# Weight blocks m, n, r first, and the state vectors' layers between the steps of tile 0's softmax

## The reference

```python
# L0: modulated attention over the heads of one token (16 heads of 32)
def modulated_linear(x, s, aff_w, aff_b, w, b):
    style = s @ aff_w.T + aff_b
    w_mod = w[None] * style[:, None, :]
    w_mod = w_mod * rsqrt(sum(w_mod * w_mod, axis=2) + EPS)[:, :, None]
    return einsum('bni,boi->bno', x, w_mod) + b
kx = modulated_linear(x, s, k...).reshape(B, N, H, D)
A = softmax(einsum('bnhd,bnjd->bnhj', kx, kx) / sqrt(D))
x = x + modulated_linear(einsum('bnhj,bnjd->bnhd', A, kx).reshape(B, N, F), s, o...)

# L1: six branches, concatenated
h = _ln(_ln(x, pw_g[pathway_ids], pw_b[pathway_ids]), cp_g[...], cp_b[...])
t = _ln(x, tm_g[time_steps], tm_b[time_steps])
m = x + _mlp_ln(memory_state, mem...)[:, None, :]      # n: noise, r: resource likewise
s = _ln(x, ms_g[scale_type], ms_b[scale_type])
w = softmax(aw)
cat = concatenate([w[0] * h, w[1] * t, w[2] * m, w[3] * n, w[4] * r, w[5] * s])
x = x + _mlp_ln(cat, int_W1, int_b1, int_W2, int_b2, int_g, int_be)
```

## Time and profile before

| | |
|---|---|
| Time, median of 3 runs | 870.54 us (870.13 to 871.36) |
| Profiled execution: its time, its span | 869.47 us, 867.6 us |
| Busy: PE, PEld | 836.8 us (96%), 731.9 us (84%) |
| Busy: DVE, ACT, POOL | 646.7 (75%), 487.6 (56%), 605.7 us (70%) |
| Chain that ended last, by engine | PE 88%, DVE 5%, DMA 2%, POOL 2%, ACT 1%, issue 1% |
| Mean granted TensorE clock | 0.989 of full speed |

### The profile page before, as it was taken

One profiled execution on the slowest core, in us unless ns is written; L12 is line 12 of the kernel. 1 busy time (PEld: TensorE's weight loads), 2 busy tenths in 40 slices (PEclk: granted clock), 3 DMA queues, 4 the chain that ended last, 5 costly groups with the idle time before them and its releaser, 6 DMA issues.

```text
span 867.6 us, 19685 instructions
## 1 busy us (share of the span) xinstructions
PE 836.8 (96%) x7456; PEld 731.9 (84%) x7474; DVE 646.7 (75%) x1067; ACT 487.6 (56%) x851; POOL 605.7 (70%) x766
## 2 busy tenths in 40 slices
PE   5996999999999999999999999999999999999997
PEld 5853888988889898888989898888988898898986
DVE  3589778778786867678797877679797767677652
ACT  3567555565656465465656556465647546464531
POOL 2367998778786767768776866668787775756472
PEclk9998999999999999999999999999999999999999
DMA  8972233424343333525243332424343342323110
GB/s 277 419 268 62 71 91 105 126 63 150 83 151 81 98 93 86 128 51 158 71 149 89 107 93 69 127 68 145 83 123 91 87 117 49 104 68 83 47 50 25
DMA packets 104365, 95.55 MB, mean 110 GB/s; under 512 B 72880, under 2 KB 78160, under 8 KB 102608
## 3 DMA queue, kind: packets, MB, share of 16 engines
q1 hardware_dynamic: 95056, 69.26, 27.7%
q0 software_dynamic: 4608, 16.78, 7.1%
q10 hardware_dynamic: 4608, 8.25, 2.8%
HBM read 69.60 MB, written 8.40 MB: 90 GB/s over the span
## 4 chain that ended last, share of the span: by engine, by line
PE 88%; DVE 5%; DMA 2%; POOL 2%; issue 1%; ACT 1%; ACTq 0%; another core or an unknown queue 0%; DVEq 0%; POOLq 0%
PE acc L405 43%; PE tok L405 28%; PE att L405 8%; PE xp L558 6%; PE xp L405 3%; DMA kb<-in_kb 1%; DVE stg_e L1284 1%; DMA pgb<-in_pw,pidx 1%; DVE raw_k L1170 0%; DVE W1xl L1274 0%; POOL op0l L1706 0%; DVE qt L1290 0%; POOL W2l L1710 0%; DVE q L1297 0%; DVE BD L1185 0%
## 5 line engine op out<-in xcount | busy, mean ns | idle before, releaser
L1706 POOL TENSOR_TENSOR op1l<-ytmp,op1h 128x512 fp32r<-128x512 f32 x64 | 89.8, 1403 | 20.1 <-ACT op1h L912 19.6
L1652 POOL TENSOR_TENSOR xlo<-xraw,xhi 128x512 fp32r<-128x512 f32 x31 | 40.5, 1306 | 68.0 <-ACT xhi L804 68.0
L405 PE MATMUL acc<-op0h,W1xh 128*128 128x256 f32 x256 | 75.8, 296 | 1.4 <-DVE op0l L1376 1.1
L405 PE MATMUL acc<-op1h,W1th 128*128 128x256 f32 x256 | 75.0, 293 | 0.0
L405 PE MATMUL acc<-op1h,W1hh 128*128 128x256 f32 x256 | 73.7, 288 | 0.0
L405 PE MATMUL acc<-op0h,W1sh 128*128 128x256 f32 x256 | 73.7, 288 | 0.0
L405 PE MATMUL acc<-op1h,W1tl 128*128 128x256 f32 x256 | 72.4, 283 | 0.0
L405 PE MATMUL acc<-op1l,W1hh 128*128 128x256 f32 x256 | 72.4, 283 | 0.0
L405 PE MATMUL acc<-op1l,W1th 128*128 128x256 f32 x256 | 72.4, 283 | 0.0
L405 PE MATMUL acc<-op0h,W1sl 128*128 128x256 f32 x256 | 72.4, 283 | 0.0
L405 PE MATMUL acc<-op1h,W1hl 128*128 128x256 f32 x256 | 72.4, 283 | 0.0
(11 more groups left out here) (269 smaller groups left out, 3005.2 us busy)
## 6 DMA issues: line engine op xcount, KB each, us to landing
xsq<-in_x SPq DMA_DIRECT2D x32, 256.0 KB, 3.1
xb<-in_x SPq DMA_DIRECT2D x32, 256.0 KB, 3.0
out<-xb SPq DMA_DIRECT2D x32, 256.0 KB, 2.4
BD<-q SPq DMA_DIRECT2D x124, 64.0 KB, 2.1
BD<-v SPq DMA_DIRECT2D x124, 64.0 KB
xraw<-in_xT SPq DMA_DIRECT2D x30, 256.0 KB, 3.0
ring<-in_k_wT ACTq DMA_DIRECT2D x6, 256.0 KB, 3.3
dmb<-dm_rows SPq DMA_DIRECT2D x6, 256.0 KB, 3.9
```

Source lines behind the costliest of these rows:

```text
L405: return e.matmul(o, a, b, start=start, stop=True, skip_group_check=True)
L1652: e.tensor_tensor(xlo[:, :, :], (xraw1 if g == 1 else xraw)[:, :, :], xhi[:, :, :].bitcast(F32), ALU.subtract).then_inc(s["xlo"], 1)
L1706: e.tensor_tensor(op[slot]["l"][:, :, half(g)], four(ytmp[YT[n, g][0]]), op[slot]["h"][:, :, half(g)].bitcast(F32), ALU.subtract).then_inc ...
```

## The change

The first-layer weights `mlp1` get a place of their own (`mlp_w1`, where the low part of `W2` is put later); block n goes straight to `stg["a"]`. The transfers of m and n go right behind that of the output weights, r behind the first-layer weights. TensorE does `mlp1` right after `proj(0)`, `mlp2` and the transposes of the demodulation behind `mod_rows(1)`, and the tables of t, s, h in three pieces; `proj(2)` follows the tables of m, n, r. ScalarE does `x_scaled`, the silu and the gain tables ahead of score_low(0). VectorE does six of the eight `x_weights` around the scores of tile 0 and the vectors ahead of `mod_first(1)`. ScalarE's split of t goes ahead of `q_hi(2)` and `e_first(1)`; GpSimd's split of t begins before root1(0).

```diff
@@
         raw["o"] = raw_o
+        mlp_w1 = at("mlp_w1", [128, 4, 512], offset=place["W2l"])
         stg = {n: at(f"stg_{n}", [128, 4, 512], offset=place[f"W{w}h"]) for n, w in zip("abcde", ("1x", "1t", "1s", "1h", "2"))}
@@
             e.dma_start(raw["o"][:, :, :], A["o_wT"]).then_inc(s["c_wo"], 16)
+            e.dma_start(raw["x"][:, :, :], A["int_w1"][2]).then_inc(s["c_rm"], 16)
+            e.dma_start(stg["a"][:, :, :], A["int_w1"][3]).then_inc(s["c_rn"], 16)
             load_sq(1)
-            e.dma_start(stg["a"][:, :, :], A["mlp1"]).then_inc(s["c_m1"], 16)
+            e.dma_start(mlp_w1[:, :, :], A["mlp1"]).then_inc(s["c_m1"], 16)
+            e.dma_start(raw["r"][:, :, :], A["int_w1"][4]).then_inc(s["c_rr"], 16)
             for i, n in enumerate(("mem", "noi", "res")):
                 e.dma_start(stg["bcd"[i]][:, :, :], A[n + "_w2"]).then_inc(s["c_w2"], 16)
-            e.dma_start(raw["x"][:, :, :], A["int_w1"][2]).then_inc(s["c_rm"], 16)
+            e.wait_ge(s["tq"], 1)
+            for i in range(3):
+                e.dma_start(rv[i][:, :], A["rows_v"][i]).then_inc(s["c_rv"], 16)
             e.dma_start(raw["t"][:, :, :], A["int_w1"][1]).then_inc(s["c_rt"], 16)
             e.dma_start(raw["s"][:, :, :], A["int_w1"][5]).then_inc(s["c_rs"], 16)
             e.dma_start(raw["h"][:, :, :], A["int_w1"][0]).then_inc(s["c_rh"], 16)
-            e.wait_ge(s["tq"], 1)
-            for i in range(3):
-                e.dma_start(rv[i][:, :], A["rows_v"][i]).then_inc(s["c_rv"], 16)
             load_tok(0)
             load_tok(1)
-            e.dma_start(raw["r"][:, :, :], A["int_w1"][4]).then_inc(s["c_rr"], 16)
             load_ids(1)
             load_sq(2)
             blocks_q(1)
+            load_tok(2)
             e.wait_ge(s["m1"], 1)
-            e.dma_start(stg["a"][:, :, :], A["int_w1"][3]).then_inc(s["c_rn"], 16)
-            load_tok(2)
             e.dma_start(raw["2"][:, :, :], A["int_w2"]).then_inc(s["c_r2"], 16)
@@
                         for c in cs:
-                            ins = mm(mlp[:, i * 16 + kt * 4:i * 16 + kt * 4 + 4], stg["a"][:, c, kt * 128:kt * 128 + 128], condT[:, c, :], start=(i == 0 and kt == 0 and c == 0))
+                            ins = mm(mlp[:, i * 16 + kt * 4:i * 16 + kt * 4 + 4], mlp_w1[:, c, kt * 128:kt * 128 + 128], condT[:, c, :], start=(i == 0 and kt == 0 and c == 0))
                 ins.then_inc(s["m1"], 1)
@@
 
-            def tables_tsh():
+            def tables_tsh(kts):
 
                 e.wait_ge(s["LB"], 3)
                 for n in "tsh":
                     e.wait_ge(s["c_r" + n], 16)
-                for kt in range(4):
+                for kt in kts:
                     for n, quarter in (("t", 0), ("s", 1), ("h", 3)):
@@
             proj(0)
+            mlp1()
             demodulation(1)
             scores(0)
             proj(1)
             mod_rows(1)
-            mlp1()
-            tables_tsh()
+            mlp2()
+            demod_T()
+            tables_tsh((0,))
             values(0)
-            demod_T()
-            mlp2()
+            tables_tsh((1, 2))
             a_T(0)
             scores(1)
+            tables_tsh((3,))
+            vec_T()
             out_proj(0)
+            tables_mnr()
             proj(2)
-            vec_T()
-            tables_mnr()
             values(1)
@@
             q_hi(0)
+            x_scaled()
             split_x(1)
             squares(1)
+            e.wait_ge(s["mh"], 1)
+            e.activation(hT[:, :, :, 0:4].rearrange("p k i b -> p i k b"), hT[:, :, :, 0:4].rearrange("p k i b -> p i k b"), ACT.Silu).then_inc(s["hs"], 1)
+            gain_tables()
             score_low(0)
@@
             e_first(0)
-            e.wait_ge(s["mh"], 1)
-            e.activation(hT[:, :, :, 0:4].rearrange("p k i b -> p i k b"), hT[:, :, :, 0:4].rearrange("p k i b -> p i k b"), ACT.Silu).then_inc(s["hs"], 1)
             split_x(2)
@@
             score_low(1)
-            x_scaled()
             exponential(1)
-            gain_tables()
             e.wait_ge(s["vTr"], 1)
             for i, n in enumerate("mnr"):
                 j = e.activation(L[n][:, :, 0:24].rearrange("p k (r c) -> p k r c", c=8)[:, :, :, 0:4],
                                  four(xp[XP["vT", 0][0]])[:, :, 32 * i:32 * i + 4].unsqueeze(2).to_broadcast([128, 4, 3, 4]), ACT.Copy, scale=w7[:, 2 + i:3 + i])
                 j.then_inc(s["LB"], 1)
-            q_hi(2)
-            e_first(1)
             e.wait_ge(s["m2"], 3)
             e.wait_ge(s["c_rt"], 16)
             split_hi(W1["t", "h"], raw["t"], s["wh"])
+            q_hi(2)
+            e_first(1)
             z_make(0)
@@
             z_copy(0)
-            e.wait_ge(s["c_rh"], 16)
-            split_hi(W1["h", "h"], raw["h"], s["wh"])
             u_make(0)
             score_low(2)
             for kt in range(4):
                 e.wait_ge(s["xc"], kt + 3)
-                e.copy(W1["x", "h"][:, kt, :], stg["e"][:, kt, :]).then_inc(s["wh"], 1)
+                e.copy(W1["x", "h"][:, kt, :], stg["e"][:, kt, :]).then_inc(s["whx"], 1)
             x1_hi(0)
+            e.wait_ge(s["c_rh"], 16)
+            split_hi(W1["h", "h"], raw["h"], s["wh"])
             x1_hi(1)
@@
                     e.wait_ge(s["c_two"], 32)
-                    e.wait_ge(s["c_L"], 1)
+                    e.wait_ge(s["c_bd"], 2)
                 w, c0, m = {"t": (1, 32, 5), "s": (5, 64, 3), "h": (0, 0, 5)}[n]
@@
                 for kt in kts:
-                    e.wait_ge(s["wh"], 4 + kt)
+                    e.wait_ge(s["whx"], kt + 1)
                     if kt == 0:
@@
             w_T(0)
+            hidden_add()
             demod_eps(1)
+            x_weights(1, (0, 1))
             score_sum(0)
             less_max(0)
+            x_weights(1, (2, 3))
+            x_weights(2, (0, 1))
             q_lo(1)
             e_T(0)
             q_T(1)
             e_second(0)
-            hidden_add()
+            vectors()
             mod_first(1, range(4))
             w_T(1)
             v_T(1)
             a_sum(0)
-            vectors()
+            vectors_norm()
             a_lo(0)
+            vectors_end()
             score_sum(1)
             less_max(1)
-            vectors_norm()
-            vectors_end()
-            x_weights(1, (0,))
+            x_weights(2, (2, 3))
             e_T(1)
             x_one(0)
             e_second(1)
             q_lo(2)
             q_T(2)
             a_sum(1)
-            x_weights(1, (1, 2))
             a_lo(1)
-            x_weights(1, (3,))
             v_stats(0)
-            x_weights(2, (0, 1, 2))
             product(0, "t")
-            x_weights(2, (3,))
             w_T(2)
@@
                 i = e.memset(L[n][:, :, :], 0.0)
-            i.then_inc(s["c_L"], 1)
+            i.then_inc(s["c_bd"], 1)
             e.wait_ge(s["c_aw"], 32)
@@
             demod(1, 1)
+            e.wait_ge(s["h2"], 3)
+            e.tensor_tensor(small[0:96, 74:75], small[0:96, 73:74], eps5[0:96, :], ALU.add).then_inc(s["lnB"], 1)
+            e.wait_ge(s["lnB"], 1)
+            e.tensor_tensor(small[0:96, 75:76], small[0:96, 74:75], mh[0:96, :], ALU.pow).then_inc(s["lnB"], 1)
             for kt in range(4):
                 mod_first_lo(kt)
             x_lo(2)
             bounds(2)
-            e.wait_ge(s["h2"], 3)
-            e.tensor_tensor(small[0:96, 74:75], small[0:96, 73:74], eps5[0:96, :], ALU.add).then_inc(s["lnB"], 1)
-            e.wait_ge(s["lnB"], 1)
-            e.tensor_tensor(small[0:96, 75:76], small[0:96, 74:75], mh[0:96, :], ALU.pow).then_inc(s["lnB"], 1)
             add_ob(0)
             true_scale(1)
             add_ob(1)
+            e.wait_ge(s["wh"], 1)
+            e.wait_ge(s["Pm"], 3)
+            split_lo(W1["t", "l"], raw["t"], W1["t", "h"], None, (0, 1))
             root1(0)
             affine(0)
             x_lo(3)
             bounds(3)
             add_ob(2)
             root2(0)
-            e.wait_ge(s["wh"], 1)
-            e.wait_ge(s["Pm"], 3)
-            split_lo(W1["t", "l"], raw["t"], W1["t", "h"], s["wlp"])
+            split_lo(W1["t", "l"], raw["t"], W1["t", "h"], s["wlp"], (2, 3))
             root1(1)
@@
                     if k == 1:
-                        e.wait_ge(s["wh"], 8)
+                        e.wait_ge(s["wh"], 4)
                         split_lo(WL["2", "l"], raw["2"], WL["2", "h"], s["wlp"], (0, 1))
                     root2(a)
                     if k == 1:

```

More of the change, by code:

```diff
@@ L24 @@
 SEMS = """
-c_abc c_aw c_one c_two c_cond c_tab c_rv c_rp c_wk c_affo c_wo c_m1 c_w2 sd sw c_rt c_rs c_rh c_rm c_rn c_rr c_r2 c_gi c_hz c_L Pc sty0 sty1
-styl st2 wsq dmm dme dbc dmb dmW stt mwh mwl sm wexp w6 t0 tp tA tB tq G m1 mh hs m2 h2 vTr LB Pm pa pT xc wh
+c_abc c_aw c_one c_two c_cond c_tab c_rv c_rp c_wk c_affo c_wo c_m1 c_w2 sd sw c_rt c_rs c_rh c_rm c_rn c_rr c_r2 c_gi c_hz Pc sty0 sty1
```

(1 more changed line is left out.)

## The result

The changed kernel takes 877.99 us (median of 5 runs, 875.86 to 878.30); the kernel before, run beside it, 870.54 us (5 runs, 870.13 to 872.37). The ratio is 1.0073, with a 95% interval of 1.0055 to 1.0091: slower by 0.7%. (The ratio is that of the means, 877.28 and 870.90 us; the medians differ by 7.4 us.) The forecast was 875.7 us, with a range of 872.5 to 879.0. The profiled execution took 876.15 us, with a span of 874.4 us.

A forecast was written before the change was run, and what follows sets the result against it. The prediction took TensorE to bound the loop and VectorE's list the prologue before the first W1_part. Terms +2.3 +1.3 +1.5 +2.0 −1.3 −0.6 give +5.2 us on the median 870.54: 875.7 us, range 872.5 to 879.0.

The forecast's parts named there:

- The place and the sign: Whole kernel: the prologue counts only through the first W1_part, 5.2 us later; slower, chance 0.86.
- one wait is left in the loop: TensorE in the loop: only one wait, 1.3 us for ScalarE's u_make(2), and it stays.
- 30.7 + 3.6 + 3.6 = 37.95 us for scores(0), +2.3 us: TensorE up to scores(0): mlp1 ahead of demodulation(1), 3.6 us each, starts scores(0) 2.3 us later.
- rival 4: Clock: TensorE idles before a_T(0), out_proj(0) runs at 1.2 GHz: +6.5, 877 us; chance 0.18 together with the port rival.
- +1.28 us for the table: ScalarE ahead of exponential(0): a second table load after the silu costs 1.28 us in full.
- +1.5 us for vectors(): VectorE's tile 0: vectors() between e_second(0) and mod_first(1), ahead of a_sum(0), adds 1.5 us.
- The wait at e_second(1): VectorE, tile 1: e_second(1) waits for q_hi(2) behind proj(2) and the tables; 3.4 us idle, 2.0 more in the sum.
- What the end gives back: Before the first W1_part: 1.3 us from x_one(1)'s slack and 0.6 us from one x_low less contended.
- Transfers at nothing: SP's queue: m, n, r early cost nothing, though t, s, h land some 3 us later.
- 1 (VectorE's list decides, faster): VectorE behind ET(0): 9.5 us off its list against 5.1 us lateness, 4.4 us faster, 866.1 us; chance 0.10.
- 2 (a small wait at e_second(1)): At e_second(1): small wait, some 2 of the 7.1 us go: +3, 873.5 us; chance 0.13.
- 3 (port): Tile 0: two x_weights queue behind GpSimd's demod steps: +7.5, 878 us; chance 0.18 together with the clock rival.

The follow-up runs named there:

- e1: The kernel before with only mlp1 moved on TensorE, right behind proj(0) and ahead of demodulation(1): 875.79 us, ratio 1.0046.
- e4: The changed kernel with twelve dense bf16 matmuls, whose output is overwritten unread, added among mlp1's: 876.43 us, ratio 1.0058.
- e7: e2 with TensorE's order also changed: values(0) earlier, the tables of t, s, h in two pieces behind proj(2): 872.08 us, ratio 1.0021.
- e5: The kernel before with one small silu of constants on ScalarE ahead of score_low(0), to price the table reload alone: 870.64 us, ratio 1.0006.
- e8: e7 with the change's order behind exponential(1) on TensorE and ScalarE: 875.10 us, ratio 1.0057.
- e2: The kernel before with the change's transfers, x_scaled ahead of score_low(0) and x_weights early; layers and later orders as before: 873.16 us, ratio 1.0023.
- e11: e3 with mlp1, silu, hidden_add, vectors and mlp2 late again, tables of t, s, h behind proj(2): 870.42 us, ratio 0.9999.
- e9: The kernel before with only blocks m and n early, r and its four adds late: 869.25 us, ratio 0.9987.
- e3: The changed kernel with the order behind exponential(1) as before, GpSimd's split of t in one piece again: 876.03 us, ratio 1.0050.
- e10: The changed kernel with the edits of e3 and e4 together: 873.00 us, ratio 1.0029.

## Why the prediction was right, and where a term was off

- **The place and the sign** were right. It is the first W1_part that counts, and the loop behind it is unchanged but for 0.3 us of a new wait. The reading that one wait is left in the loop was wrong, though: there are two, the second of 1.1 us, in both kernels, so it cancels.
- **"30.7 + 3.6 + 3.6 = 37.95 us for scores(0), +2.3 us"** is the term that was mis-sized: it measured +6.4. The missing 4.1 us are 3.2 us of demodulation(1) at 1.2 GHz (6.83 against 3.64) and 0.9 us by which proj(0) ended later (31.60 against 30.73). I took both durations from rows at 2.4 GHz and put the clock only as rival 4, ahead of a_T(0) and out_proj(0). e1 shows the place of mlp1 as the cause, e4 the clock. Why proj(0) kept 1.2 GHz longer is open. Its end varies between kernels anyway: 30.27 us in e7 and 31.28 in e5, with mlp1 late in both.
- **+1.28 us for the table** was right: exponential(0) came 1.54 us later than scores(0) did, e1 and e5 give 1.35 and 1.29. By the rule quoted there (the Trainium skill, ScalarE: Activation LUTs, What ACT_TABLE_LOAD costs) another 1.38 us would have followed; no load in these traces shows it.
- **+1.5 us for vectors()** ahead of a_sum(0): ET(0) came another 1.38 us later.
- **The wait at e_second(1)** (forecast 3.4 us idle, 2.0 us beyond ET(0)'s delay) measured 3.73 and 1.2, so this term was 0.8 us too large. e8 against e7 confirms its cause, the file of tables, proj(2) and q_hi(2).
- **What the end gives back** was too small: −1.3 and −0.6 were forecast, −2.4 and −2.0 measured. I had VectorE's slack and one x_low in it, but not TensorE's clock. out_proj(1) took 3.5 us before (78.90 to 82.41), partly at 1.2 GHz, and 3.0 us now; x_T(1) with proj(3) 3.9 us before (88.04 to 91.91) and 2.6 us now (95.45 to 98.04). These are 1.8 of the 2.5 us.
- **Transfers at nothing:** right for the changed kernel (h landed at 48.5, the tables began at 53.90, kb took 12.3 us), though h came 5.1 us later and not some 3 (two blocks of 1 MB at the 401 GB/s used for kb would have said 5.2), and only since mlp2 stands ahead of the tables. e2 shows the price without that cover: 3.75 us.
- **Rivals.** 1 (VectorE's list decides, faster) was wrong; the list is worth 2.4 to 3.1 us in the profiled executions of e11, e9 and e2, of which the medians show 0.2 (e11) and 1.4 (e9), not 9.5 less 5.1. 2 (a small wait at e_second(1)) was wrong: 3.73 us. 3 (port) was wrong: beside demod two x_weights took 1.41 us. 4 (clock) was right as a mechanism, wrong in its place.

Two errors (the first term too small by 4.1 us, the end by 2.5) partly cancel; the sum of 5.2 us against 6.1 at W1 looks better than its parts, and that it does is luck. In the medians the loss is 7.4 us. 6.7 of them lie between the two profiled executions; the rest is their spread.

## What to carry to other kernels

Before moving a block of very narrow matmuls next to another, price both at the lower clock too: without a gap between them they can still lose it, and what waits behind pays double. Ask of each gain in a prologue whether it survives the next place where TensorE waits: in e3's profiled execution a gain of 1.3 us was gone twelve matmuls later. And cut a change of this kind in its parts: at the first W1_part the early blocks gained 2.4 us (e11 against before) and the early layers lost 8.3 (e3 against e11). Then hold the parts against the medians, which show 5.6 us lost and no gain beyond the noise (0.2 us).

## What was unexpected of the hardware

- TensorE's clock fell while the engine was busy without a gap: behind the 32 fp32 matmuls of 128x4 of mlp1 the next 32 took 6.83 us instead of 3.64, with the engine busy for 10.00 of 10 us and the granted clock 0.75 (30 to 40 us; in e1 9.93 and 0.70). With twelve 128x512 bf16 matmuls among mlp1's the next 32 took 3.49 us (e4, granted clock 1.00), and the clock fell behind them. The Trainium skill (TensorE: Matmul & The Clock Gate, Part 1) ties the clock to how busy the engine has been recently; the profile's busy share in these rows does not show the fall.
- The same twelve matmuls of out_proj(1) took 3.0, 4.5 and 5.1 us in the changed kernel, e3 and e10, which differ only in what ran before.
- A table load of 1.28 us is followed by its ACTIVATE within 0.02 us where the input is there (48.96 and 50.26 here, 43.12 and 44.41 in e5).
- Beside GpSimd's 128x512 steps (in e7 the output weights' split until 56.39, then x_lo, 1.73 us from 56.35) two x_weights took 3.19 us; beside its steps of 12 elements a partition 1.41 us, no more than twice the 0.74 us of a step alone.
